# The last stage of a 2,048-token kernel in 16 units of 256 columns in place of 8 of 512

## What is computed

```python
v = 0; integrated = xf                       # (2048, 128)
for _ in range(2):                           # NUM_ITER
    ctx = concat([integrated, v])
    shared = gelu(ctx @ w_s1 + b_s1) @ w_s2 + b_s2          # 64 hidden, 3*128 out
    for each of the 2 chosen experts of a token:
        ctrl = gelu(ctx @ w1[e] + b1[e]) @ w2[e] + b2[e]    # 64 hidden, 3*128 out
    # each control gives alpha, beta, gate:
    #   v' = sigmoid(alpha)*v - softplus(beta)*(integrated - mu)
    #   x' = integrated + 0.1*sigmoid(gate)*v'
    x_next, v_next = mix of the shared and the two expert results
    halt = sigmoid(gelu(x_next @ w_h1 + b_h1) @ w_h2 + b_h2)
    refined = gelu(x_next @ w_f1 + b_f1) @ w_f2 + b_f2
    integrated = integrated + halt * refined * integration_weight
    v = v_next
return x + integrated
```

## Time and profile before

| | |
|---|---|
| median of 3 runs | 2280.06 us (2272.35 to 2289.49) |
| the profiled execution | 2283.65 us, of which the span in the profile is 2281.9 us |
| this stage in the span | from 1948.7 us to the end, 333.2 us |
| busy in the whole span | PE 80%, DVE 68%, ACT 61% |

### The profile page before, as it was taken

One profiled execution on the slowest core, in us unless ns is written; L12 is line 12 of the kernel. 1 busy time (PEld: TensorE's weight loads), 2 busy tenths in 40 slices (PEclk: granted clock), 3 DMA queues, 4 the chain that ended last, 5 costly groups with the idle time before them and its releaser, 6 DMA issues. The chain is left out here.

```text
span 2281.9 us, 32065 instructions
## 1 busy us (share of the span) xinstructions
PE 1823.7 (80%) x10443; PEld 761.7 (33%) x10446; DVE 1552.8 (68%) x1549; ACT 1398.3 (61%) x2920; POOL 676.2 (30%) x369
## 2 busy tenths in 40 slices
PE   6799999976886666766666887379998985999985
PEld 1333333333333333333332343124333333333331
DVE  6788888816999999999995322456555634465463
ACT  2377777757999999999993132225454553443432
POOL 1000000003999999999994001100000000000000
PEclk8799999987978887788787988569898896899996
DMA  4211121004666665666661010242232000000000
GB/s 146 54 25 25 25 40 20 2 10 139 208 203 207 200 200 196 196 200 201 199 202 42 27 47 1 72 74 50 39 48 42 16 1 15 0 0 0 0 5 14
DMA packets 56962, 182.30 MB, mean 80 GB/s; under 512 B 8373, under 2 KB 11728, under 8 KB 55312
## 3 DMA queue, kind: packets, MB, share of 16 engines
q1 hardware_dynamic: 56200, 179.74, 26.9%
q10 hardware_dynamic: 648, 1.04, 0.2%
HBM read 160.56 MB, written 7.21 MB: 74 GB/s over the span
## 5 line engine op out<-in xcount | busy, mean ns | idle before, releaser
L680 DVE TENSOR_REDUCE attn_mx<-banks 128x1 f32<-128x1024 f32 (+7 forms) x512 | 502.4, 990 | 180.7 <-PE banks L485 121.7
L630 ACT ACTIVATE attn_probs<-banks 128x512 f32<-128x512 f32 (+3 forms) x896 | 446.0, 550 | 282.2 <-PE banks L513 181.8
L1753 POOL TENSOR_TENSOR hc<-st,ct 128x1024 f32<-128x1024 f32 x256 | 598.7, 2366 | 46.3 <-DVE st L1711 46.2
L1711 DVE TENSOR_TENSOR_SCAN st<-da,banks 128x1024 f32<-128x1024 f32 x256 | 566.6, 2269 | 19.6 <-DVE banks L1703 13.2
L1676 ACT ACTIVATE ut<-b_turned,x_now 128x128 f32<-128x128 f32 x1280 | 389.8, 388 | 2.9 <-PE banks L1569 1.2
L513 PE MATMUL banks<-attn_qa,attn_ka 99*128 99x512 bf16 (+3 forms) x896 | 274.1, 375 | 21.1 <-DMA attn_qa<-attn_mrow 19.0
L1668 ACT ACTIVATE da<-dt,a_now 128x1024 f32<-128x1024 f32 x256 | 284.2, 1138 | 10.6 <-DVE st L1711 8.9
L1569 PE MATMUL banks<-mats,ut 128*128 128x128 f32 x1280 | 237.8, 328 | 58.4 <-DVE st L1711 38.4
L533 PE MATMUL banks<-attn_probs,attn_vst 128*32 128x256 f32 (+3 forms) x3584 | 273.4, 376 | 4.1 <-ACT attn_osb L621 3.8
L483 PE MATMUL banks<-attn_ka,attn_qa 64*128 64x512 bf16 (+3 forms) x512 | 203.1, 397 | 77.1 <-DMA attn_ku<-attn_ka 55.6
L1592 PE MATMUL banks<-hc,onecol 128*32 128x512 f32 x1024 | 182.8, 795 | 97.8 <-POOL onecol L1744 89.0
(11 more groups left out here) (422 smaller groups left out, 1850.4 us busy)
## 6 DMA issues: line engine op xcount, KB each, us to landing
dt<-dt_rows SPq DMA_DIRECT2D x256, 512.0 KB, 4.5
attn_qa<-q_lin SPq DMA_DIRECT2D x144, 64.0 KB
attn_qu<-attn_qa SPq DMA_DIRECT2D x16, 512.0 KB, 4.2
moe_w<-in_moe_w SPq DMA_DIRECT2D x2, 2048.0 KB, 10.1
attn_ka<-k_lin SPq DMA_DIRECT2D x63, 64.0 KB
mats<-in_mats SPq DMA_DIRECT2D x1, 2844.5 KB, 15.0
attn_ku<-attn_ka SPq DMA_DIRECT2D x8, 256.0 KB, 5.0
q_lin<-qparts SPq DMA_DIRECT2D x6, 256.0 KB
```

Source lines behind the costliest of these rows:

```text
L630: nc.scalar.activation(probs[s % 4][:, jj, c0:BLK], scores_exp[jj][:, c0:BLK], ACT.Exp, scale=scale).then_inc(probs_ready, 1)
L680: nc.vector.reduce_max(mx[:, qt, j:j + 1], scores_max[n % 2][:, 0:w], AX.X)\
L1711: nc.vector.tensor_tensor_scan(st[n % 4][:, :], da[n % 4][:, :], pair[:, :, :].rearrange("p h t -> p (h t)"), 0.0, ALU.mult, ALU.add).then ...
L1753: nc.gpsimd.tensor_tensor(hc[n % 8][:, :], st[n % 4][:, :], ct[:, b * SEQ:(b + 1) * SEQ], ALU.mult)\
```

## The change

The block width of `refine` becomes W = 256 and the number of blocks NB = 8, so NU goes from 8 to 16. Every tile of the stage has half its columns, each product, activation and DVE operation is issued twice as often on half the columns, and the output is sent in eight pieces in place of four. The order of the engines within a unit, the buffers' numbers and the bank rotation are as before; PSUM banks are used for half their columns. Nothing outside the stage is touched.

```diff
-    NU = 2 * NBLK
+    W = 256
+    NB = T // W
+    NU = 2 * NB
     PAIRS = EXPERTS // 2
+    bank = [k.bank[i][:, 0:W] for i in range(8)]
...
-    hid = k.sb("hid", [128, PAIRS, BLK], ctx=ctx)
+    hid = k.sb("hid", [128, PAIRS, W], ctx=ctx)
...
-    raw = k.sb("beta_raw", [128, 3, BLK], ctx=ctx)
-    beta = [k.sb(f"beta{i}", [128, 3, BLK], ctx=ctx) for i in range(2)]
+    raw = k.sb("beta_raw", [128, 3, W], ctx=ctx)
+    beta = [k.sb(f"beta{i}", [128, 3, W], ctx=ctx) for i in range(2)]
...
-    hidden_bank = k.bank[0:2]
-    control_bank = k.bank[2:6]
+    hidden_bank = bank[0:2]
+    control_bank = bank[2:6]
 
     def second(u):
-        return u >= NBLK
+        return u >= NB
 
     def cols(u):
-        return sl(u % NBLK)
+        return sl(u % NB, W)
...
                 if second(u):
-                    pe.wait_ge(xi_ready, u - NBLK + 1)
-                    pe.wait_ge(v_ready, u - NBLK + 1)
+                    pe.wait_ge(xi_ready, u - NB + 1)
+                    pe.wait_ge(v_ready, u - NB + 1)
...
-            for b in blocks(T):
+            for b in range(NB):
                 sp.wait_ge(y_ready, b + 1)
-                sp.dma_start(y[:, sl(b)], k.x[:, sl(b)]).then_inc(y_sent, 16)
-            sp.wait_ge(y_sent, 16 * NBLK)
+                sp.dma_start(y[:, sl(b, W)], k.x[:, sl(b, W)]).then_inc(y_sent, 16)
+            sp.wait_ge(y_sent, 16 * NB)
```

More of the change, by code:

```diff
@@ L2221, in refine @@
     nc = k.nc
-    NU = 2 * NBLK
+    W = 256
+    NB = T // W
+    NU = 2 * NB
     PAIRS = EXPERTS // 2
+    bank = [k.bank[i][:, 0:W] for i in range(8)]
     SHARED = 2
     v = k.sb("vel", [128, T], ctx=ctx)
-    hid = k.sb("hid", [128, PAIRS, BLK], ctx=ctx)
-    hid_s = [k.sb(f"hid_s{i}", [EH, BLK], ctx=ctx) for i in range(2)]
-    hid_m = [k.sb(f"hid_m{i}", [128, 2, PAIRS, BLK], ctx=ctx) for i in range(2)]
-    raw = k.sb("beta_raw", [128, 3, BLK], ctx=ctx)
-    beta = [k.sb(f"beta{i}", [128, 3, BLK], ctx=ctx) for i in range(2)]
[L2231 to L2240, removed]
+    hid = k.sb("hid", [128, PAIRS, W], ctx=ctx)
+    hid_s = [k.sb(f"hid_s{i}", [EH, W], ctx=ctx) for i in range(2)]
+    hid_m = [k.sb(f"hid_m{i}", [128, 2, PAIRS, W], ctx=ctx) for i in range(2)]
+    raw = k.sb("beta_raw", [128, 3, W], ctx=ctx)
+    beta = [k.sb(f"beta{i}", [128, 3, W], ctx=ctx) for i in range(2)]
+    alpha = k.sb("alpha", [128, 3, W], ctx=ctx)
+    gate = [k.retired(3 * W * i, 3 * W).rearrange("p (s f) -> p s f", f=W) for i in range(2)]
+    err = [k.sb(f"err{i}", [128, W], ctx=ctx) for i in range(2)]
+    sum_a = k.sb("sum_a", [128, W], ctx=ctx)
+    sum_b = k.sb("sum_b", [128, W], ctx=ctx)
+    xn = k.sb("x_next", [128, W], ctx=ctx)
+    hh = k.sb("halt_hid", [32, W], ctx=ctx)
+    fh = k.sb("ref_hid", [128, 2, W], ctx=ctx)
+    halt = k.sb("halt", [128, W], ctx=ctx)
+    ref = k.sb("refined", [128, W], ctx=ctx)
     hid_scored = k.sem("hid_scored")
@@ L2290, in taken @@
             return gate_ready, 3 * u + s + 1
-        return alpha_ready, 3 * (u - NBLK) + s + 1
+        return alpha_ready, 3 * (u - NB) + s + 1
     with nc.Block() as block:
@@ L2338, in halt_first @@
                     pe.wait_ge(halt_ready, u)
-                nc.tensor.matmul(k.bank[6][0:32, :], k.m("w_h1"), xn[:, :], start=True, stop=True)\
+                nc.tensor.matmul(bank[6][0:32, :], k.m("w_h1"), xn[:, :], start=True, stop=True)\
                     .then_inc(halt_scored, 1)
-                nc.tensor.matmul(k.bank[7][:, :], k.m("w_f1", lo=0, n=128), xn[:, :], start=True, stop=True)\
+                nc.tensor.matmul(bank[7][:, :], k.m("w_f1", lo=0, n=128), xn[:, :], start=True, stop=True)\
                     .then_inc(halt_scored, 1)
@@ L2345, in halt_second @@
                 pe.wait_ge(halt_hid, 3 * u + 1)
-                nc.tensor.matmul(k.bank[6][:, :], k.m("w_f1", lo=128, n=128), xn[:, :], start=True, stop=True)\
+                nc.tensor.matmul(bank[6][:, :], k.m("w_f1", lo=128, n=128), xn[:, :], start=True, stop=True)\
                     .then_inc(halt_scored, 1)
@@ L2350, in halt_third @@
                 pe.wait_ge(halt_hid, 3 * u + 2)
-                nc.tensor.matmul(k.bank[7][:, :], k.m("w_h2", 32).to_broadcast([32, 128]), hh[:, :], start=True,
+                nc.tensor.matmul(bank[7][:, :], k.m("w_h2", 32).to_broadcast([32, 128]), hh[:, :], start=True,
                                  stop=True).then_inc(halt_scored, 1)
@@ L2356, in halt_last @@
                 for c in range(2):
-                    last = nc.tensor.matmul(k.bank[6][:, :], k.m("w_f2", lo=c * 128, n=128), fh[:, c, :], start=c == 0,
+                    last = nc.tensor.matmul(bank[6][:, :], k.m("w_f2", lo=c * 128, n=128), fh[:, c, :], start=c == 0,
                                             stop=c == 1)
@@ L2419, in alphas @@
             def alphas(u, s):
-                if s == 0 and u > NBLK:
+                if s == 0 and u > NB:
                     act.wait_ge(xn_ready, u)
@@ L2439, in halt_gelu @@
                 if n == 0:
-                    nc.scalar.activation(hh[:, :], k.bank[6][0:32, :], ACT.Gelu, bias=k.c("b_h1", 32))\
+                    nc.scalar.activation(hh[:, :], bank[6][0:32, :], ACT.Gelu, bias=k.c("b_h1", 32))\
                         .then_inc(halt_hid, 1)
                 else:
-                    nc.scalar.activation(fh[:, n - 1, :], k.bank[8 - n][:, :], ACT.Gelu, bias=k.c(f"b_f1_{n - 1}"))\
+                    nc.scalar.activation(fh[:, n - 1, :], bank[8 - n][:, :], ACT.Gelu, bias=k.c(f"b_f1_{n - 1}"))\
                         .then_inc(halt_hid, 1)
@@ L2449, in halt_gate @@
                     act.wait_ge(xi_ready, u)
-                nc.scalar.activation(halt[:, :], k.bank[7][:, :], ACT.Tanh, bias=hb2[:, :], scale=0.5)\
+                nc.scalar.activation(halt[:, :], bank[7][:, :], ACT.Tanh, bias=hb2[:, :], scale=0.5)\
                     .then_inc(halt_ready, 1)
@@ L2536, in step_ahead @@
                 nc.vector.tensor_tensor(b[:, :, :], b[:, :, :], g[:, :, :], ALU.mult)
-                dve.wait_ge(alpha_ready, 3 * (u - NBLK) + 3)
+                dve.wait_ge(alpha_ready, 3 * (u - NB) + 3)
                 link(nc.vector.scalar_tensor_tensor(a[:, :, :], a[:, :, :], 1.0, g[:, :, :], ALU.add, ALU.mult))
@@ L2553, in halting @@
                 dve.wait_ge(halt_scored, 5 * u + 5)
-                link(nc.vector.tensor_scalar(ref[:, :], k.bank[6][:, :], k.c("b_f2"), k.c("iw"), ALU.add, ALU.mult))
+                link(nc.vector.tensor_scalar(ref[:, :], bank[6][:, :], k.c("b_f2"), k.c("iw"), ALU.add, ALU.mult))
                 dve.wait_ge(halt_ready, u + 1)
```

## The result

The changed kernel takes 2312.67 us (median of 4 runs, 2301.99 to 2315.44), the kernel before 2282.45 in the same comparison: a ratio of 1.0127, 95% interval 1.0076 to 1.0178. It is slower, by 30 us at the medians; the forecast was 2310. The profiled execution took 2315.44 us, its span is 2313.6.

The account below looks back on a forecast made before the run. PE was taken to bound the steady part; start 32.5, 13 steps 269.4 and drain 62.0 sum to 363.9 us against 333.2, +30.7, so 2310 us, 1.3% slower; forecast's own range 2298 to 2324, 8 in 10 2288 to 2334.

Parts of the forecast that it names:

- PE bounds the steady part, which can only lose: Middle 180.8 us of the last stage: PE busy 177.8, 3 us idle to give back; only start and drain can gain.
- Price of the columns: PE instructions: 0.83 ns per column, 256 fewer save 0.212 us per float32 instruction; an expert group falls from 3.95 to 2.15.
- Hidden: Hidden products on PE in each step, with ACT's table load and Gelu: 4.45 us first pass, 6.0 second pass.
- DVE keeps up with 1.0 us of slack: DVE's chain to `xi`, awaited by PE's halt_first: 7.7 us against PE's 8.75, so the wait costs nothing.
- ACT's other two loads are covered: Table loads before L2433 and L2450 in each unit: covered by PE's work, with 1.8 us left.
- Start: First stretch of the stage, up to the first halt_first: 55.8 us becomes 32.5.
- Drain: Last stretch of the stage, from 2185.32: 96.6 us becomes 62.0, 34.6 less.
- PE's stretch between DVE's two chains: In the drain, 2225.15 to 2242.87, over half of it at half clock: 17.7 us becomes 12.0 (10.4 to 13.5).
- DVE's second piece: In the drain, DVE's work to 2263.4, some 11,800 columns: 15.5 us becomes 9.1.
- Leftovers that shrink: Rival: what stays around waits halves with the columns, group 1.98 us, time 2276 (half-way 2293), not slower; 20%.
- DVE as the bound: Rival: chain to `xi` takes 9.6 instead of 7.7 us, PE waits 1 us at each of 14 halt_first: 2324; 8%.
- The clock: Rival: PE's clock falls at each of eight first-pass units, 3 to 4 us each, 32 at most: 2342; 12%.

Follow-up runs that it names:

- the second execution: The changed kernel (256 columns) run again with nothing altered, to see whether the clock's fall comes back: 2308.5 us, ratio 1.0158.

## Why the prediction was right, step by step

- **PE bounds the steady part, which can only lose.** Right: its idle time went from 3 to 16.5 us.
- **Price of the columns.** Predicted 2.15 us for a group, 17.49, 19.04 and 23.96 for the steps; measured 2.13, 17.45, 18.98 and 23.87. The 13 steps: 269.4 predicted, 269.7 measured, 1.3 of which is the clock's fall, which I had left out of the forecast; without it they are 1.0 under my sum.
- **Hidden.** 4.45 and 6.0 predicted, 4.46 and 5.99 measured, pauses of 1.49 and 1.06 us. The table load stands there as assumed, shown by taking it out; so does the wait of the last product.
- **DVE keeps up with 1.0 us of slack.** Measured 1.0, for a chain of 7.7 us as predicted. (The mask that I read DVE's 1.06 ns per column from gives 1.10, 4.49 us for 4,096 columns; 8,192 columns at either value give the same slack within 0.2 us.) That it is a real edge was shown when the load was taken out: 0.35 us of wait per step.
- **ACT's other two loads are covered.** Right at 256 (ACT is idle 1.69 us before hidden's load), and gone at 128.
- **Start.** 32.5 predicted, 34.2 measured: the clock rose at 1958.4, later than at 512 columns (1954.9), so a whole expert group ran at half clock. This lay in the bounds I gave. In the second execution the start took 32.3. The 3.15 us for its second hidden stage stood in my sum without a working; it took 3.17.
- **Drain.** 62.0 predicted, 60.9 measured. Most of that is PE's stretch between DVE's two chains, 10.6 instead of 12.0 us, at half clock only until 2283.3. The table load that came into the chain, which I had not priced, made DVE's second piece 9.55 instead of 9.1; no other term is off by more than 0.4.
- **Rivals.** Leftovers that shrink: excluded by the two kernels without the bf16 product and by the group at 128 columns. DVE as the bound: no wait at 256. The clock: I gave it 12% for a fall in every unit; it fell once in each of two executions, so the mechanism is there, at 1.3 us of the 32 I had priced. By my own list of signs a clock under 1.0 in the steady part spoke against the forecast, and it was 0.99. At 128 columns it becomes the largest part of my error: the first-pass steps at full clock would take 154 us and took 191.4.

## What to carry to other kernels

Narrower units pay only for the time in which the bounding engine stands idle at the ends of a pipeline, and every pause, every fixed piece beside streaming and every table load in its path is paid again for each new unit: count those first, at their present length. If the gain sought is in the drain, look whether an order written for the last unit gets it at the wide size; here that gave 23.9 us where halving the units cost 31.6. When a wait is taken out of a loop, the next chain (here DVE's, 1.0 us behind) tells how much of it is kept.

## What the runs showed of the hardware

The clock of TensorE did not fall at pauses of 1.28 us in steps of 29.8 us, fell once in 270 us at pauses of 1.49 us in steps of 17.4, three times in 14 steps of 15.0 us at pauses of 1.46, and was 0.76 in the mean at pauses of 1.6 to 1.9 us in steps of 12 to 17. An expert group showed the same 0.32 us beside its streaming at 512 and at 256 columns and 0.34 at 128, 0.2 of it for one bf16 product ahead of float32 ones. An ACT table load took 1.28 us at every width, and which set is loaded for a Tanh decides whether the next Gelu needs another (48 loads in this stage at 256 columns, 33 with the Gelu table loaded by name).
